# Grouped attention: DVE splits the keys in slot 0, takes the two largest logits in slot 1 and selects in slot 2

## The chip, the cores and the metric

One Trainium2 chip, one core of it. The metric is the device time of one execution of the whole program in microseconds (us). Durations of single instructions come from one profiled execution.

## What is computed

The program is a chain of two layers over 16 chunks of 512 tokens with 128 features. The change lies in the second step of the first layer: attention with 16 query heads over 4 key heads of 8 features each, then the routing of each token to two of eight experts. Cut to what matters here:

```python
q = rope((h @ Wq).reshape(b, s, 16, 8))
k = rope((h @ Wk).reshape(b, s, 4, 8))
scores = where(causal, q @ repeat(k, 4).T / sqrt(8), min)
h = clip(residual + softmax(scores) @ v @ Wo, -100, 100)
logits = rmsnorm(h) @ Wr                       # 8 experts
topv, topi = top_k(softmax(logits), 2)         # the two largest
w = sum(one_hot(topi) * topv / sum(topv))
```

## The kernel before

`grouped_attention` runs the engines by five programs written out by hand, one instruction list each, tied by semaphores. The outer loop is a pass b from -1 to 16, and a pass has eight slots s from 0 to 7. In a slot, TensorE (PE) computes the scores of one pair of heads of chunk b in three parts (`score`) and, eleven pairs ahead, the same products for the row maxima in three parts (`max_scores`); VectorE (DVE) reduces the latter (`take_max`, lines 791, 794 and 798) and ScalarE (ACT) takes exponentials of the former. Three pairs of PSUM banks go round between the two kinds, so that PE's second `score` after a `max_scores` waits until DVE has reduced it. One further bank, M, serves everything else in turn.

Around this, each slot holds pieces of work for other chunks. Those that matter here, by slot, with c2 = b + 2 the chunk whose queries and keys are prepared and r = b - 2 the chunk that is routed:

- Slot 0: GpSimd (POOL) adds the two halves of the rotated queries (`rotate`, line 636), ACT copies the keys (`copy_sum`), and DVE behind its three `take_max` splits the queries of c2 into bfloat16 parts (`split_q`, lines 779 to 783). POOL makes the third part in slot 1 (`third_q`, then `third_k`).
- Slot 1: PE multiplies the rows of chunk r with the router (`turn_h`, `route`); at the slot's end DVE copies the logits (`take_logits`, line 844) and then splits the keys of c2 (`split_k`, lines 768 to 772).
- Slot 2: DVE combines a group of the attention's output, and at the slot's end runs `choose`: the eight largest per token (line 851), their indices (line 854), the gap (line 857), and the selection matrix `sel` (line 867).
- Slot 3: PE multiplies `sel` (`rank`, line 304) between `score` parts 1 and 2, DVE runs `place`, and at the end `shift`.
- Slot 4: `max_scores` starts on the first head pair of chunk c2. Its first instruction (line 325) waits until the queries and keys of that chunk have been loaded.

The DMA queue of SyncE (SP) carries this, in order, once per pass: `store_q` (lines 1008 to 1012, waits for the split queries), `store_k` (lines 1018 to 1020, waits for the split keys), `load_q` (line 1027, waits until the queries' stores have landed), `load_k` (line 1034, waits until the keys' stores have landed), then the row maxima. In the printed rows ga_q, ga_k and g_q, g_k are buffers of the same ring of three.

Of the kernel before, what the change touches and what calls it, by code (L numbers as in the profile page):

```python
# [47 lines left out]
def grouped_attention(nc, C, XT, H, G, T, R, NB):  # L48
# [15 lines left out]
    with ExitStack() as ctx:  # L64
# [118 lines left out]
        def exists(c):  # L183
            return 0 <= c < NB
# [545 lines left out]
        def dve_program(v):  # L730
# [21 lines left out]
            def sines(c):  # L752
                v.wait_ge(qs_filled, c)
                if c > 1:
                    v.wait_ge(q_split, c - 1)
                v.tensor_tensor(rotB[:, :], M[:, :], rope[:, 1, :], ALU.mult).then_inc(sin_done, 1)

            def rotate_k(c):
                v.wait_ge(kk_filled, c)
                v.tensor_tensor(rotK[:, :], M[0:2 * KV * HD, :], k_rope[:, :], ALU.mult  # L760
                                ).then_inc(kk_done, 1)

            def split_k(c):

                v.wait_ge(sum_copied, c)
                if c > 1:
                    v.wait_ge(k_stored, 48 * (c - 1))
                v.tensor_copy(partsK[:, 0, :], restK[:, :])
                v.drain()
                v.tensor_tensor(restK[:, :], restK[:, :], partsK[:, 0, :], ALU.subtract)  # L770
                v.drain()
                v.tensor_copy(partsK[:, 1, :], restK[:, :]).then_inc(k_two, 1)

            def split_q(c):

                v.wait_ge(rotated, c)
                if c > 1:
                    v.wait_ge(q_stored, 48 * (c - 1))
                v.tensor_copy(partsQ[:, 0, :], rotA[:, :])
                v.drain()  # L780
                v.tensor_tensor(rotB[:, :], rotA[:, :], partsQ[:, 0, :], ALU.subtract)
                v.drain()
                v.tensor_copy(partsQ[:, 1, :], rotB[:, :]).then_inc(q_two, 1)

            def take_max(n, part):
                u = 3 * n + part
                v.wait_ge(max_filled, u + 1)
                h = 2 * (n % 8)
                blocks = max_banks(u).rearrange("p i (a n) -> p i a n", n=P)
                if part == 0:  # L790
                    v.tensor_reduce(bm[:, h:h + 2, 0:16:5], blocks, AX.X, ALU.max  # L791
                                    ).then_inc(max_taken, 1)
                elif part == 1:
                    v.tensor_reduce(  # L794
                        bm[:, h:h + 2, 8:14].rearrange("p i (a n) -> p i a n", n=3)[:, :, :, 0:2],
                        blocks, AX.X, ALU.max).then_inc(max_taken, 1)
                else:
                    v.tensor_reduce(bm[:, h:h + 2, 4], max_banks(u)[:, :, 0:256], AX.X, ALU.max
                                    ).then_inc(max_taken, 1)
# [18 lines left out]
            def combine(b, g):  # L818

                v.wait_ge(o_turned, 4 * b + g + 1)  # L820
                o = M[:, :].rearrange("p (a d) -> p a d", d=32)
                v.reciprocal(rsum[:, :], o[:, :, VD])
                v.drain()
                if g == 0 and b:
                    v.wait_ge(yT_filled, b)
                lanes = y[:, :, 4 * VD * g:4 * VD * (g + 1)].rearrange("p t (c d) -> p t c d", d=VD)
                shares = rsum[:, :].rearrange("p (t c) -> p t c", t=NT).unsqueeze(3)
                last = v.tensor_tensor(lanes, o[:, :, 0:VD].rearrange("p (t c) d -> p t c d", t=NT),
                                       shares.to_broadcast([P, NT, 4, VD]), ALU.mult)
                last.then_inc(o_used, 1)  # L830
                if g == 3:
                    v.wait_ge(o_used, 4 * b + 4)
                    v.sem_inc(y_ready, 1)
# [8 lines left out]
            def take_logits(r):  # L842
                v.wait_ge(logits_filled, r + 1)
                v.tensor_copy(logit[:, :, :], M[:, 0:NT * E].rearrange("p (t e) -> p t e", t=NT)
                              ).then_inc(logits_taken, 1)

            def choose(r):

                v.drain()
                for t in range(NT):  # L850
                    v.max(top[:, t, :], logit[:, t, :])
                v.drain()
                for t in range(NT):
                    v.max_index(topi[:, t, :], top[:, t, :], logit[:, t, :])
                if r >= 2:
                    v.wait_ge(ratio_ready, r - 1)
                v.tensor_tensor(gap[:, r % 2, :], top[:, :, 1], top[:, :, 0], ALU.subtract
                                ).then_inc(gap_ready, 1)
                v.drain()
                v.tensor_copy(topf[:, :, :].rearrange("p j t -> p t j"), topi[:, :, 0:2])  # L860
                v.drain()
                v.tensor_tensor(one[:, :, :, :].rearrange("p j t e -> p (j t) e"),
                                C["iota8"][:, :].unsqueeze(1).to_broadcast([P, 2 * NT, E]),
                                topf[:, :, :].rearrange("p j t -> p (j t)").unsqueeze(2
                                ).to_broadcast([P, 2 * NT, E]), ALU.is_equal)
                v.drain()
                v.tensor_tensor(sel[:, :, :], one[:, 0, :, :], one[:, 1, :, :], ALU.add
                                ).then_inc(sel_ready, 1)

            def place(r):  # L870

                v.wait_ge(ranks_filled, r + 1)
                v.tensor_tensor(pos[:, :, :], M[:, 0:NT * E].rearrange("p (t e) -> p t e", t=NT),
                                run[:, :].unsqueeze(1).to_broadcast([P, NT, E]), ALU.add)
                v.drain()
                v.tensor_tensor(run[:, :], run[:, :], M[:, NT * E:NT * E + E], ALU.add
                                ).then_inc(ranks_taken, 1)
                for j in range(2):
                    v.tensor_tensor(one[:, j, :, :], one[:, j, :, :], pos[:, :, :], ALU.mult)
                v.drain()  # L880
                v.tensor_reduce(slotf[:, :, :], one[:, :, :, :], AX.X, ALU.add)
                v.drain()
                if r >= 2:
                    v.wait_ge(scattered[r % 2], 16 * 2 * NT * (r // 2))
                v.tensor_copy(R["slot"][:, r % 2, :, :], slotf[:, :, :]).then_inc(slots_ready, 1)
# [71 lines left out]
            for b in range(-1, NB + 1):  # L957
                p, c, c2, c3, r = b - 1, b + 1, b + 2, b + 3, b - 2
                for s in range(8):
                    m = 8 * b + s + 1 + AHEAD  # L960
                    scanning = 0 <= m < 8 * NB and b > -2
                    if scanning:
                        take_max(m, 0)
                    if s == 0 and exists(p):
                        combine(p, 2)
                    if s == 2 and exists(p):
                        combine(p, 3)
                    if s == 3 and exists(r):
                        place(r)
                    if s == 4 and exists(b):  # L970
                        combine(b, 0)
                    if s == 6 and exists(b):
                        combine(b, 1)
                    if s == 7 and exists(c3):
                        sines(c3)
                    if scanning:
                        take_max(m, 1)
                    if scanning:
                        take_max(m, 2)
                    if s == 0 and exists(c2):  # L980
                        split_q(c2)
                    if s == 4 and exists(p):
                        add_out(p)
                    if s == 6 and exists(c3):
                        cosines(c3)
                    if s == 7 and exists(c3):
                        rotate_k(c3)
                    if s == 1 and exists(r):
                        take_logits(r)
                    if s == 1 and exists(c2):  # L990
                        split_k(c2)
                    if s == 2 and exists(r):
                        choose(r)
                    if s == 5 and 3 <= b + 4 < NB:
                        measure(b + 4)
                    if s == 3 and exists(c):
                        shift(c)
                    if s == 7 and b == NB - 1:
                        count_whole()
                    if s == 0 and b == NB:  # L1000
                        plan_whole()
# [2864 lines left out]
```

## Time and profile before

| | us |
|---|---|
| median of 3 runs | 3178.02 |
| their lowest and highest | 3171.54, 3179.92 |
| the profiled execution's own time | 3179.74 |
| its span, first to last instruction | 3178.0 |

The span is 1.74 us below that execution's own time. The grouped attention lies between about 538 and 1291 us of the span. Times in the timeline are from the span's start; "idle before" in brackets is the time for which the engine stood still ahead of the instruction, with what ended it; "issue" there means nothing that the profile shows. The granted clock is a share of TensorE's full 2.4 GHz; its other level is half of that.

### The profile page before, as it was taken

What the parts mean: (1) busy time and instruction counts of PE and PEld (TensorE: products, weight loads), DVE (VectorE), ACT (ScalarE), POOL (GpSimd) and SP (SyncE); (2) the same over time, 40 slices, a digit from 0 to 9 for tenths busy, and PEclk for the clock granted to TensorE, in tenths of its full rate; (3) what the DMA queues carried; (4) which work ended last, traced back from release to release, by engine and by line L of the source; (5) the groups of instructions that cost most, each with busy time, mean ns of one, the idle gap of its engine ahead of it and who ended that gap; (6) DMA issues with size and microseconds to landing.
All of it is one profiled execution on the core that took longest, in us unless ns stands there. A gap on an engine that the chain in (4) does not pass through costs nothing. (4 is left out here: it accounts for less than half of the span.)

```text
span 3178.0 us, 66212 instructions
## 1 busy us (share of the span) xinstructions
PE 2909.8 (92%) x22258; PEld 1849.4 (58%) x22258; DVE 2457.0 (77%) x6944; ACT 2327.2 (73%) x3601; POOL 2096.7 (66%) x2402
## 2 busy tenths in 40 slices
PE   6999997689898888789579999999999999999979
PEld 3555554344444444678346666666666666666658
DVE  5666665778788885567568888888888888888867
ACT  5777874356666667444279999999999999999933
POOL 5565664345565643577658877877878788778744
PEclk8999998799999999899789999999999999999989
DMA  4434444223223320585400000000000000000001
GB/s 121 130 98 121 112 104 94 59 59 69 56 61 70 69 68 24 170 276 164 135 1 1 17 1 16 2 7 11 1 17 1 17 1 17 1 17 1 1 14 41
DMA packets 151509, 178.31 MB, mean 56 GB/s; under 512 B 18619, under 2 KB 122784, under 8 KB 151076
## 3 DMA queue, kind: packets, MB, share of 16 engines
q1 hardware_dynamic: 142084, 157.14, 18.9%
q0 software_dynamic: 9088, 16.94, 1.5%
q8 instruction: 179, 2.93, 0.4%
q14 instruction: 158, 1.29, 0.1%
HBM read 99.82 MB, written 75.95 MB: 55 GB/s over the span
## 5 line engine op out<-in xcount | busy, mean ns | idle before, releaser
L3377 PE MATMUL lb_FF<-lb_h,lb_w 128*128 128x512 f32 x1024 | 501.1, 592 | 0.0
L3606 DVE TENSOR_SCALAR lb_z<-lb_M,lb_mv,lb_rstd 128x128 f32<-128x128 f32 x1024 | 344.9, 398 | 3.3 <-POOL lb_rstd L3531 3.0
L3494 ACT ACTIVATE lb_h<-lb_H,lb_prm 128x512 f32<-128x512 f32 x512 | 327.5, 699 | 2.5 <-PE lb_H L3368 2.5
L3531 POOL TENSOR_TENSOR lb_rstd<-lb_rstd,half 128x4 f32<-128x4 f32 x256 | 260.8, 1019 | 37.3 <-issue 1.3
L3362 PE MATMUL lb_H<-lb_x1s,lb_w 128*128 128x512 f32 x512 | 272.9, 533 | 0.8 <-issue 0.8
L3377 PEld LDWEIGHTS lb_FF<-lb_h,lb_w 128*128 128x128 f32 x1024 | 193.4, 189 | 89.9 <-issue 61.1
L1575 ACT ACTIVATE da_PT<-da_SY 128x1536 f32<-128x1536 f32 x128 | 185.3, 1447 | 73.5 <-PE da_SY L1424 73.3
L3598 DVE BATCH_NORM_STATS2 lb_stats<-lb_M 128x6 f32<-128x128 f32 x1024 | 226.9, 284 | 14.8 <-PE lb_M L3321 8.8
L1653 POOL TENSOR_SCALAR_AFFINE_SELECT da_PT<-da_PT 128x1024 f32<-128x1024 f32 x128 | 141.6, 1112 | 133.5 <-ACT da_PT L1570 133.5
L3363 PE MATMUL lb_H<-lb_x1s,lb_w 128*128 128x512 f32 x512 | 203.0, 397 | 0.0
L3368 PE MATMUL lb_H<-lb_x1s,lb_w 128*128 128x512 f32 x512 | 202.7, 397 | 0.0
L1436 PE MATMUL da_O<-da_PT,da_V 128*32 128x128 f32 (+2 forms) x3584 | 192.2, 326 | 2.6 <-DVE da_oT L1824 2.1
L3549 POOL CAST lb_x1s<-lb_x 128x512 fp32r<-128x512 f32 x128 | 78.3, 611 | 174.0 <-DVE lb_x L3631 174.0
L2628 POOL DMA_INDIRECT moe_ys<-moe_y,moe_dest x156 | 159.2, 1021 | 49.8 <-issue 45.8
L794 DVE TENSOR_REDUCE ga_bm<-ga_S 128x8 f32<-128x1024 f32 x128 | 156.5, 1223 | 42.9 <-PE ga_S L379 41.3
L791 DVE TENSOR_REDUCE ga_bm<-ga_S 128x8 f32<-128x1024 f32 x128 | 155.9, 1218 | 43.3 <-PE ga_S L379 42.9
L3542 POOL TENSOR_TENSOR lb_xs<-H,lb_xs 128x512 fp32r<-128x512 f32 x126 | 167.8, 1332 | 18.1
L3552 POOL TENSOR_TENSOR lb_x1s<-lb_x,lb_x1s 128x512 fp32r<-128x512 f32 x128 | 163.4, 1276 | 20.8 <-issue 20.8
L3563 POOL TENSOR_TENSOR lb_y<-lb_ao,H 128x512 f32<-128x512 f32 x128 | 165.4, 1292 | 16.2 <-ACT lb_ao L3481 14.0
L3575 POOL TENSOR_TENSOR lb_y<-lb_ff,lb_x 128x512 f32<-128x512 f32 x128 | 165.1, 1290 | 8.3 <-PE lb_M L3321 5.8
L3475 ACT ACT_TABLE_LOAD x131 | 168.1, 1283 | 2.3
L3452 ACT ACT_TABLE_LOAD x128 | 164.2, 1283 | 2.3
(514 smaller groups left out, 8774.8 us busy)
## 6 DMA issues: line engine op xcount, KB each, us to landing
moe_w<-experts_dram SPq DMA_DIRECT2D x39, 384.0 KB, 3.1
da_qT<-da_stq SPq DMA_DIRECT2D x64, 192.0 KB, 3.9
da_kT<-da_stk SPq DMA_DIRECT2D x64, 192.0 KB, 3.4
moe_x<-moe_xs SPq DMA_DIRECT2D x39, 260.0 KB, 3.6
tc_g<-moe_ys SPq DMA_DIRECT2D x32, 256.0 KB, 3.3
ga_q<-ga_stq SPq DMA_DIRECT2D x20, 384.0 KB, 5.9
lb_split<-moe_parts SPq DMA_DIRECT2D x8, 896.0 KB, 6.1
da_stq<-da_parts SPq DMA_DIRECT2D x16, 384.0 KB, 2.4
```

The costliest lines, as they stand in the source:

```text
L1436: last = pe.matmul(O[32 * c:32 * c + 32, q0:q0 + cols], V[:, (n // 4) % 2, j, 2 * (n % 4) + c % 2, :], PT[:, (2 * n + c // 2) % RING, c % ...
L1575: act.activation(PT[:, n % RING, :, 512:HEAD_COLS], SY[:, :, :].rearrange("p a n -> p (a n)").rearrange("p (i n) -> p i n", i=2), ACT.Exp, ...
L3362: pe.matmul(H[:, k % 2, :], w1[:, 0, k, :], x1s[:, 0, :], start=True, stop=False)
L3363: pe.matmul(H[:, k % 2, :], w1[:, 1, k, :], x1s[:, 0, :], start=False, stop=False)
L3368: pe.matmul(H[:, k % 2, :], w1[:, 0, k, :], x1s[:, 1, :], start=False, stop=True).then_inc(h_filled, 1)
L3377: pe.matmul(FF[:, :], w2[:, k, :], h[:, k, :], start=(k == 0), stop=(k == KC - 1)).then_inc(ff_filled, 1)
L3475: act.preload_act_table_set("gelu_apprx_tanh_and_others")
L3494: act.activation(h[:, k, :], H[:, k % 2, :], ACT.Gelu_apprx_tanh, bias=col(FB1 + k, i)).then_inc(h_ready, 1)
L3531: pool.tensor_tensor(out[:, :], out[:, :], C["half"][:, 0:NT], ALU.pow).then_inc(done, 1)
L3542: pool.tensor_tensor(part_of_x(i, 1), state(i), part_of_x(i, 0).bitcast(F32), ALU.subtract).then_inc(xs_ready, 1)
L3598: v.bn_stats(stats[:, t, :], M[:, t * P:(t + 1) * P])
L3606: last = v.tensor_scalar(z[:, t, :], M[:, t * P:(t + 1) * P], mv[:, t, 0:1], rstd[:, t:t + 1], ALU.subtract, ALU.mult)
```

## The change

On DVE alone, three things move. `split_k` goes from the end of slot 1 to the end of slot 0, directly behind `split_q`. The search for the largest logits and their indices goes from `choose` at the end of slot 2 to `take_logits` at the end of slot 1, behind a drain of its own. `choose` keeps the gap, the selection and a drain ahead of them. No instruction is dropped; one drain per routed chunk is added. The lists of the other engines and of SP stay.

```diff
                 v.tensor_copy(logit[:, :, :], M[:, 0:NT * E].rearrange("p (t e) -> p t e", t=NT)
                               ).then_inc(logits_taken, 1)
+                v.drain()
+                for t in range(NT):
+                    v.max(top[:, t, :], logit[:, t, :])
+                v.drain()
+                for t in range(NT):
+                    v.max_index(topi[:, t, :], top[:, t, :], logit[:, t, :])
 
             def choose(r):
 
                 v.drain()
-                for t in range(NT):
-                    v.max(top[:, t, :], logit[:, t, :])
-                v.drain()
-                for t in range(NT):
-                    v.max_index(topi[:, t, :], top[:, t, :], logit[:, t, :])
                 if r >= 2:
                     v.wait_ge(ratio_ready, r - 1)
...
                         rotate_k(c3)
+                    if s == 0 and exists(c2):
+                        split_k(c2)
                     if s == 1 and exists(r):
                         take_logits(r)
-                    if s == 1 and exists(c2):
-                        split_k(c2)
                     if s == 2 and exists(r):
                         choose(r)
```

## Rows read from the trace of the kernel before

**Rows 1.** The page, part 1: busy time, share of the span, instructions.

```profile
PE 2909.8 (92%) x22258; PEld 1849.4 (58%) x22258; DVE 2457.0 (77%) x6944; ACT 2327.2 (73%) x3601; POOL 2096.7 (66%) x2402
```

**Rows 2.** Waits of PE from 600 to 1176: sum in us, times, longest.

```profile
PE ga_S L325 <- issue: 21.6, 12, 4.5
PE ga_S L355 <- DVE ga_bm L791: 14.4, 16, 1.7
PE ga_M L304 <- DVE g_sel L867: 13.7, 11, 1.7
```

**Rows 3.** Timeline of pass 10, from its slot 0 to its slot 4.

```profile
1042.15 0.43 DVE L779 CAST ga_partsQ<-ga_rotA 128x512 bf16<-128x512 f32 x1 [1.02 <-POOL ga_rotA L636]
...
1043.76 1.22 DVE L791 TENSOR_REDUCE ga_bm<-ga_S 128x8 f32<-128x1024 f32 x1
...
1045.03 0.28 PE L355 MATMUL ga_S<-ga_q,ga_k 51*128 51x256 bf16 x2 [1.10 <-DVE ga_bm L791]
...
1046.06 1.80 SPq L1012 DMA_DIRECT2D ga_stq<-ga_partsQ  x1
...
1046.72 0.40 DVE L768 CAST ga_partsK<-ga_restK 32x512 bf16<-32x512 f32 x1
...
1048.29 1.21 DVE L791 TENSOR_REDUCE ga_bm<-ga_S 128x8 f32<-128x1024 f32 x1
...
1049.63 0.32 SPq L1018 DMA_DIRECT2D ga_stk<-ga_partsK  x1
...
1050.98 0.89 SPq L1027 DMA_DIRECT2D g_q<-ga_stq  x2
...
1052.04 0.83 SPq L1034 DMA_DIRECT2D g_k<-ga_stk  x2
...
1052.09 0.37 DVE L851 MAX8 g_top<-g_logit 128x8 f32<-128x8 f32 x4
...
1053.10 0.15 DVE L857 TENSOR_TENSOR g_gap<-g_top 128x4 f32<-128x4 f32 x1
...
1054.22 0.18 PE L304 MATMUL ga_M<-g_sel,g_matsb 128*128 128x32 bf16 x1 [1.27 <-DVE g_sel L867]
...
1059.97 0.39 PE L325 MATMUL ga_S<-identb,half_masks 64*128 64x256 bf16 x4 [1.89 <-issue]
```

**Rows 4.** DMA issues from 600 to 1170: KB each, median us to landing.

```profile
ga_k<-ga_stk SPq DMA_DIRECT2D x18, 192.0 KB, 7.2
...
ga_stq<-ga_partsQ SPq DMA_DIRECT2D x13, 128.0 KB, 2.7
```

**Rows 5.** Timeline: PE at slot 4 of pass -1 and of pass 1.

```profile
580.71 0.61 PE L325 MATMUL ga_S<-identb,half_masks 64*128 64x256 bf16 x4 [8.68 <-DMA ga_k<-ga_stk]
...
663.85 0.61 PE L325 MATMUL ga_S<-identb,half_masks 64*128 64x256 bf16 x4 [4.30 <-issue]
```

**Rows 6.** Stretches: length, busy PE, PEld, DVE, ACT, POOL, clock, DMA, GB/s.

```profile
690.16:1175.70 485.54, 433.66 (x5396) 224.40 (x5396) 400.69 (x862) 309.73 (x740) 283.86 (x385) 0.95 0.29 65
929.84:954.87 25.03, 24.55 (x312) 12.09 (x312) 20.86 (x37) 17.58 (x45) 15.96 (x20) 1.00 0.09 27
1059.97:1086.56 26.59, 26.11 (x312) 12.71 (x312) 20.36 (x35) 16.77 (x43) 14.94 (x20) 0.94 0.08 26
957.76:968.27 10.51, 9.42 (x113) 6.06 (x114) 8.61 (x28) 6.02 (x13) 5.75 (x11) 0.84 0.66 156
1045.03:1054.22 9.19, 7.91 (x112) 5.16 (x113) 8.42 (x28) 6.03 (x14) 4.43 (x10) 1.00 0.59 157
870.58:882.64 12.06, 10.84 (x112) 6.98 (x113) 8.84 (x28) 6.15 (x14) 6.41 (x12) 0.72 0.64 146
```

**Rows 7.** Timeline of the last pass: DVE's logits and their search.

```profile
1279.99 0.19 DVE L844 COPY g_logit<-ga_M 128x32 f32<-128x32 f32 x1 [0.98 <-PE ga_M L295]
...
1283.17 0.37 DVE L851 MAX8 g_top<-g_logit 128x8 f32<-128x8 f32 x4 [0.20 <-DVE ga_y L828]
```

More of the change, by code:

```diff
@@ L845, in take_logits @@
                               ).then_inc(logits_taken, 1)
-            def choose(r):
                 v.drain()
@@ L854, in choose @@
                     v.max_index(topi[:, t, :], top[:, t, :], logit[:, t, :])
+            def choose(r):
+                v.drain()
                 if r >= 2:
```

## The prediction

> **What bounds the kernel now.** I read the page first: PE is busy for 92% of the span and DVE for 77% [rows 1], so that neither alone explains a stage. The edit touches only the grouped attention, so I went to the waits of PE inside that stage, then to the timeline of one pass, then to the DMA issues, and last to stretches with their granted clock. Three waits of PE stand out [rows 2]. The largest is at line 325, where `max_scores` meets a new chunk in slot 4: 21.6 us in 12 of 13 passes, put down to "issue". The next are PE in slot 1 on DVE's `take_max` (14.4 us) and PE in slot 3 on the selection matrix (13.7 us in 11 passes, 1.25 each).
>
> What is behind "issue"? In pass -1 the same wait is put down to the load of the keys [rows 5]. In pass 10, SP issues the two key loads from 1052.04 on, the second some 0.4 us later, and a key load lands 7.2 us after its issue [rows 4]: 1059.65, against PE's start at 1059.97 [rows 3]. So PE waits for the keys. They are late because DVE splits them only at 1046.72, at the end of slot 1.
>
> So a pass is a loop with a gate. Counted from line 779 of pass 10 (1042.15), PE resumes in slot 1 at 2.88, reaches `rank` at 12.07, arrives at the gate at 15.93 and passes it at 17.82 [rows 3]. From the gate to the next pass's line 779 it is 25.03 us at full clock in pass 7 and 26.59 us in pass 10, whose clock was 0.94 there [rows 6]. The mean pass from 2 to 12 takes 485.54 / 11 = 44.14 us [rows 6].
>
> **The change part by part.** *Keys in slot 0.* The split of the keys occupies DVE for 1.57 us (1046.72 to 1048.29, the next `take_max`) [rows 3]. Placed at 1043.76 it delays all three `take_max` of slot 1 by that much, and PE's wait in slot 1, on the first of them, grows from 1.10 to 2.67: PE resumes at 4.45. Behind it on DVE stand those reductions and the logits; behind them wait PE's `score` part 2 and `route`, and ACT's last exponentials. The keys' copy by ACT is an earlier piece of the same slot and has the 1.61 us of the query split as cover; without cover its lateness would add to this delay.
>
> *Search in slot 1.* From line 851 to line 857 it is 1.01 us [rows 3]; with the new drain I take 1.1 (below, a drain costs nothing and it is 1.0; above, 0.3 like the gaps between the dependent steps of `choose` would make it 1.3). It takes the place of the 1.57 us at the end of slot 1, so that slot 2's first `take_max` is late by 1.57 - 1.57 + 1.1 = 1.1 or so on DVE's own account, while PE offers its input 1.57 late. In slot 2, PE is therefore the one that sets the pace, at +1.57. At the end of slot 2, DVE is about 1.33 behind, the search is gone, and the gap comes at 1.33 - 1.01 = 0.32 later than now. The selection is ready at 12.07 + 0.33 = 12.4.
>
> *Slot 3.* PE needs 9.19 us from its start in slot 1 to `rank`, 1.27 of them wait [rows 3, 6]. 4.45 + 7.92 = 12.37: the wait on the selection disappears, as PE itself comes 1.57 later. Up to the gate it is another 3.86 us, so PE arrives at 16.26 rather than 15.93. Alone, the regrouping on DVE thus moves a wait from slot 3 to slot 1 and costs 0.33 us a pass. ACT's ratio and POOL's row weights come later by the same amount, and no other engine waits on those before the scatter.
>
> *What the earlier keys trigger.* From line 768 to the first store it is now 2.91 us [rows 3]; from 1043.76 that gives 1046.67. SP is then still in `store_q`, whose last issue starts at 1046.06. The key stores take 1.35 us of SP's time, but `load_q` behind them also needs the queries landed, 2.7 us after their last issue [rows 4], at 1048.76. So the loads start at 1048.8, not 1050.98: 2.15 us earlier. Bounds: 1.75 if SP's last query store always takes the 1.80 us of this pass, 2.9 if the landing were no limit. The gate opens at 17.82 - 2.15 = 15.67, at most 16.07: before PE is there.
>
> *The clock.* A longer stop may drop it. From PE's start in slot 1 to `rank`, pass 10 had clock 1.00 and took 9.19 us, pass 8 had 0.84 and 10.51, pass 6 had 0.72 and 12.06 [rows 6]. Without the wait on the selection these are 7.92, 9.26 and 10.81, so the arrivals are 16.26, 17.57 and 19.12. Passes of 41.3, 42.6 and 44.15 us follow with 25.03 us behind the gate, as pass 7 has where the gate held PE little. The Trainium skill (TensorE: Matmul & The Clock Gate, section "HAM oscillation — how this bites in real kernels") warns that a wait which recurs at every tile throttles PE anew at every tile. By that rule every pass would pay; the trace agrees for passes 6 and 8, not for pass 10, which waited as long. By the rule alone the whole would come to 3153, by pass 10's row to 3137.
>
> *The sum.* I take low clock once in ten of passes 2 to 13 (42.6, each 1.54 less) and the longer kind in two (no gain): -15.4. Passes -1 to 1 route nothing and wait 8.68, 4.5 and 4.30 at the gate [rows 2, 5]; more than the 1.57 by which PE can come later, so each gains the 2.15 of the load: -6.5. In the last three passes no keys are split. In the last, the logits are there at 1279.99 but the search starts at 1283.17, behind `combine` [rows 7]: 1.0 us leaves the chain. The same 1.0 leaves pass 14's selection wait, and pass 15 I cost at nothing, as ACT's exponentials cover it: -2.0. The profiled execution took 3179.74: less 23.9 it is 3156. (The median of the runs is 1.7 lower; I leave that in the range.)
>
> **The rivals.** About 0.3%, 9.5 us, is what a measurement of this kernel tells from no change.
>
> *No low clock in slots 1 and 2.* 41.3 a pass: 12 x 2.84 = 34, with the other 8.5 it is 3137. For it speaks pass 10; against it that the wait is 2.4 times as long.
>
> *The longer low clock in every pass*, as in pass 6, whose wait of 1.7 was the longest of its kind [rows 2]: 44.15, so passes 2 to 13 gain nothing and only 8.5 remain: 3171. It speaks for it that this is the one pass with a longer wait, against it that the clock was low from the wait's end on there, so may have been cause as much as effect.
>
> *The load does not come forward*, because the stores of queries and keys now share the queue and land later. The gate stays at 17.82: passes of 42.85 (low clock ahead of it) to 44.41, about 0.5 gained in each, and nothing in the first three: 3172. Against it: stores and loads of one pass never overlap, since `load_q` waits for the landing.
>
> *Slower: the clock falls twice a pass.* The slot 1 wait brings the long kind (44.15) and another stretch falls low behind the gate, at 26.59 - 25.03 = 1.56 more [rows 6]: 45.7, or +18.8 in twelve passes, less 8.5: 3190. It decides from a mean clock of about 0.89 over passes 2 to 12, against 0.95 now. Against it: behind the gate it was the stop at the gate that preceded the fall, and that stop goes.
>
> **How the numbers follow.** The forecast's case (3145 to 3168 by itself) has 0.50, no low clock 0.10, the longer low clock 0.22, the unmoved load 0.08, the slower case 0.10. The faster ones are the first two, 0.60; the next two lie within 0.3%, 0.30; slower 0.10. The range leaves out the slower case and most of the 3137 case: 3141 to 3180.
>
> **What would show it.** The wait of PE in slot 1 near 2.7 us (line 355 on line 791); no wait on the selection before `rank`; "issue" at line 325 close to nothing from pass 2 on and about 2 us shorter in passes -1 to 1; line 1034 about 7.7 us behind line 779, from 9.89; passes near 42.6 us. The forecast is wrong if the gate's wait stays, if the clock over passes 2 to 12 leaves 0.92 to 0.98, or if a later stage takes back what this one gains.

## The result, and the profile after

The changed kernel takes 3185.85 us (median of 7 runs, 3181.76 to 3195.03) against 3175.28 (7 runs, 3171.24 to 3179.92): a ratio of 1.0034, 95% interval 1.0021 to 1.0047. It is slower by 10.6 us, just beyond what a measurement tells from no change; forecast were 3156 and a range of 3141 to 3180. The profiled execution, the longest of the seven, took 3195.03 (span 3193.3) against 3179.74.

First the waits of PE in the changed kernel from 600 to 1176, as in [rows 2].

```profile
PE ga_S L355 <- DVE ga_bm L791: 49.8, 26, 3.7
PE ga_S L325 <- DVE ga_bm L794: 7.5, 14, 0.7
...
PE ga_M L304 <- DVE g_sel L868: 0.4, 1, 0.4
```

Two of the three waits of [rows 2] are gone, as forecast: "issue" at line 325 (21.6 us) and the selection (13.7, now 0.4). But the wait in slot 1 has grown from 14.4 to 49.8 us, by 35.4, which is as much as the two together. The timeline of pass 10 shows how it is made up (from line 844 on, lines after the moved search stand one lower than before, so load_k is line 1035 and the selection 868).

```profile
1052.15 0.43 DVE L779 CAST ga_partsQ<-ga_rotA 128x512 bf16<-128x512 f32 x1 [0.99 <-POOL ga_rotA L636]
...
1053.75 0.41 DVE L768 CAST ga_partsK<-ga_restK 32x512 bf16<-32x512 f32 x1
1053.92 1.26 POOL L640 TENSOR_TENSOR ga_partsQ<-ga_rotB,ga_partsQ 128x512 bf16<-128x512 f32 x1 [1.80 <-DVE ga_partsQ L783]
1054.24 1.48 DVE L770 TENSOR_TENSOR ga_restK<-ga_restK,ga_partsK 32x512 f32<-32x512 f32 x1
...
1056.13 1.21 DVE L791 TENSOR_REDUCE ga_bm<-ga_S 128x8 f32<-128x1024 f32 x1
...
1057.40 0.28 PE L355 MATMUL ga_S<-ga_q,ga_k 51*128 51x256 bf16 x2 [3.43 <-DVE ga_bm L791]
...
1061.31 0.79 SPq L1035 DMA_DIRECT2D g_k<-ga_stk  x2
...
1066.91 0.18 PE L304 MATMUL ga_M<-g_sel,g_matsb 128*128 128x32 bf16 x1
...
1070.16 0.39 PE L325 MATMUL ga_S<-identb,half_masks 64*128 64x256 bf16 x4 [0.55 <-DVE ga_bm L794]
...
1070.61 0.39 PE L325 MATMUL ga_S<-identb,half_masks 64*128 64x256 bf16 x4
...
1073.85 0.28 PE L355 MATMUL ga_S<-ga_q,ga_k 51*128 51x256 bf16 x2 [0.50 <-DVE ga_bm L791]
...
1096.49 0.43 DVE L779 CAST ga_partsQ<-ga_rotA 128x512 bf16<-128x512 f32 x1 [1.01 <-POOL ga_rotA L636]
```

PE resumes in slot 1 at 5.25 from line 779 (forecast 4.45) after a stop of 3.43 (forecast 2.67), reaches `rank` at 14.76 without a wait, and the pass takes 44.34. The gate is the instruction at 1070.61, and it starts without a wait. (The one at 1070.16, on the same line, belongs to the `score` ahead of it and waits for a reduction of DVE.) In pass -1 the gate still holds PE, for 5.87 us instead of 8.68 [rows 5]:

```profile
579.86 0.61 PE L325 MATMUL ga_S<-identb,half_masks 64*128 64x256 bf16 x4 [5.87 <-DMA ga_k<-ga_stk]
```

Next stretches of the changed kernel, columns as in [rows 6]: passes 2 to 12; from PE's start in slot 1 to `rank` in passes 10, 9 and 8 (that of pass 8 begins 0.04 us early); from `rank` to the next line 779 in pass 10.

```profile
684.10:1185.17 501.07, 443.84 (x5396) 232.68 (x5396) 409.86 (x862) 310.36 (x740) 284.00 (x385) 0.93 0.28 63
1057.40:1066.91 9.51, 9.43 (x113) 6.09 (x113) 7.29 (x25) 5.01 (x11) 6.17 (x12) 0.82 0.90 173
1011.93:1022.53 10.60, 10.51 (x112) 6.94 (x113) 7.39 (x25) 5.01 (x11) 6.18 (x12) 0.72 0.89 163
965.02:977.11 12.09, 11.64 (x113) 7.04 (x114) 7.43 (x25) 5.34 (x12) 6.21 (x12) 0.65 0.78 145
1066.91:1096.49 29.58, 27.93 (x360) 13.74 (x360) 24.99 (x49) 20.95 (x53) 17.27 (x22) 1.00 0.10 27
```

Read the column of the granted clock (0.93 for passes 2 to 12, from 0.95): PE is busy nearly without a gap behind the stop, yet it needs 9.51 to 12.09 us for the same work, since part of it runs at the lower level of 1.2 GHz. The eleven passes take 501.07 instead of 485.54: 45.55 each, not 44.14. Passes -1 to 1 fell from 127.55 to 120.93, and the time from pass 13's line 779 to the start of the last addition of the output (line 839) from 114.41 to 111.27. Together the attention, up to that addition, ends 6.3 us later (1296.44, from 1290.11).

The remainder is at the other end of the program, in code that the diff does not touch. The last stage, from the last use of `lb_H` to the end of the span, takes 157.1 us instead of 149.5. Here are two groups of its instructions, first before, then after (busy time, mean of one, idle time ahead):

```profile
L3038 POOL TENSOR_TENSOR ff_r<-ff_r 128x512 f32<-128x512 f32 x32 | 44.2, 1395 | 29.1 <-ACT ff_r L3020 29.0
L3064 DVE TENSOR_SCALAR ff_xn<-XT,ff_mv,ff_rstd 128x128 f32<-128x128 f32 x56 | 17.9, 383 | 10.5 <-POOL ff_rstd L3030 10.5
```

```profile
L3039 POOL TENSOR_TENSOR ff_r<-ff_r 128x512 f32<-128x512 f32 x32 | 38.4, 1204 | 29.6 <-ACT ff_r L3021 29.6
L3065 DVE TENSOR_SCALAR ff_xn<-XT,ff_mv,ff_rstd 128x128 f32<-128x128 f32 x56 | 24.6, 502 | 11.9 <-POOL ff_rstd L3031 11.9
```

The same 56 instructions of DVE take 24.6 us, not 17.9, while POOL's squares got shorter. The timeline of the changed kernel there shows why:

```profile
3133.04 1.84 DVE L3065 TENSOR_SCALAR ff_xn<-XT,ff_mv,ff_rstd 128x128 f32<-128x128 f32 x4 [0.89 <-POOL ff_rstd L3031]
...
3133.73 1.06 POOL L3039 TENSOR_TENSOR ff_r<-ff_r 128x512 f32<-128x512 f32 x1 [0.73 <-ACT ff_r L3021]
...
3134.93 0.66 PE L2965 MATMUL ff_M<-ident,ff_xn 128*128 128x128 f32 x4 [0.54 <-DVE ff_xn L3065]
```

POOL's square falls beside DVE's four normalisations (1.84 us). In the kernel before it fell behind them (1.12 for the same four) and beside DVE's own squares (line 3087):

```profile
3093.63 1.12 DVE L3064 TENSOR_SCALAR ff_xn<-XT,ff_mv,ff_rstd 128x128 f32<-128x128 f32 x4 [0.68 <-POOL ff_rstd L3030]
...
3094.66 2.13 DVE L3087 TENSOR_TENSOR ff_r<-ff_r 128x512 f32<-128x512 f32 x2
...
3094.76 2.93 POOL L3038 TENSOR_TENSOR ff_r<-ff_r 128x512 f32<-128x512 f32 x2 [1.17 <-ACT ff_r L3020]
```

PE waits on line 3065 ten times, for 8.4 us in all, where it waited twice, for 2.7.

### The profile page after: what moved, and what is told of

It is laid out like the page before. It is cut to its first block and busy times, and to the rows that moved or that the text cites. A ratio compares the mean times of both kernels' runs of the same rounds, so it can differ in the third digit from the quotient of the medians.

```text
span 3193.3 us, 66227 instructions
## 1 busy us (share of the span) xinstructions
PE 2920.9 (91%) x22258; PEld 1856.9 (58%) x22258; DVE 2474.6 (77%) x6944; ACT 2327.9 (73%) x3601; POOL 2090.4 (65%) x2402
## 5 line engine op out<-in xcount | busy, mean ns | idle before, releaser
L3599 DVE BATCH_NORM_STATS2 lb_stats<-lb_M 128x6 f32<-128x128 f32 x1024 | 226.8, 283 | 13.9 <-PE lb_M L3322 8.9
L794 DVE TENSOR_REDUCE ga_bm<-ga_S 128x8 f32<-128x1024 f32 x128 | 156.2, 1220 | 36.9 <-PE ga_S L379 36.6
```

Source lines behind the costliest of these rows:

```text
L3599: v.bn_stats(stats[:, t, :], M[:, t * P:(t + 1) * P])
```

## The experiments

**Half of the change each.** First the search alone, moved to slot 1; the keys are split behind it.

```diff
                               ).then_inc(logits_taken, 1)
+                v.drain()
+                for t in range(NT):
+                    v.max(top[:, t, :], logit[:, t, :])
+                v.drain()
+                for t in range(NT):
+                    v.max_index(topi[:, t, :], top[:, t, :], logit[:, t, :])
             def choose(r):
                 v.drain()
-                for t in range(NT):
-                    v.max(top[:, t, :], logit[:, t, :])
-                v.drain()
-                for t in range(NT):
-                    v.max_index(topi[:, t, :], top[:, t, :], logit[:, t, :])
```

> Kernel before with the search alone moved to slot 1, ahead of the key split, which stays in slot 1. If the cost of the change lies in the key split's new place (position theory) or in the overlap of its subtraction with POOL's third query part (overlap theory), this kernel lacks both: line 770 stays at 0.68 us, the stop of PE in slot 1 stays at 1.1, the wait on the selection before rank shrinks. But the keys are then split 1.1 us later, so the gate in slot 4 opens 1.1 us later and passes 2 to 13 take about 45.2 instead of 44.1: 3175 + 13 - 2 = 3186 (ratio 1.003). If it is the search in slot 1 that costs (rival), the loss comes without a later gate: a new stop of PE in slot 2 and a gate with no longer a wait.

3207.59 us (4 runs, 3202.44 to 3211.13), ratio 1.0093 (1.0076 to 1.0110), and so slower still than the 3186 expected. Timeline of pass 10 (its line 779 is at 1063.95): key split, load of the keys, gate.

```profile
1069.70 0.40 DVE L768 CAST ga_partsK<-ga_restK 32x512 bf16<-32x512 f32 x1
...
1075.02 0.83 SPq L1035 DMA_DIRECT2D g_k<-ga_stk  x2
...
1083.00 0.61 PE L325 MATMUL ga_S<-identb,half_masks 64*128 64x256 bf16 x4 [2.78 <-issue]
```

The loads start at 11.07 (9.89 before) and the gate opens at 19.05 (17.82). That is the forecast's loop of keys and gate, turned against the kernel: 1.2 us later in, 1.2 us later out. The passes grew by 2.57 (46.71), so the stop of 2.78 cost more than its lateness; the clock over passes 2 to 12 was 0.91. No new stop came in slot 2 (PE's waits on line 794 sum to 8.5 us, 8.6 before), so the rival, which put the loss on the search itself, falls.

Then the split alone, moved to slot 0.

```diff
                     if s == 0 and exists(c2):
                         split_q(c2)
...
+                    if s == 0 and exists(c2):
+                        split_k(c2)
                     if s == 1 and exists(r):
                         take_logits(r)
-                    if s == 1 and exists(c2):
-                        split_k(c2)
```

> Kernel before with the key split alone moved to slot 0; the search stays in slot 2. Position and overlap theories: stop of PE in slot 1 of 3.45 us as in the changed kernel, line 770 at 1.48, no wait at the gate from pass 0 on, and the wait on the selection before rank back at about 1, so that passes take up to 1.1 us more than in the changed kernel: 45.4 to 47, in all 3186 to 3200. The search rival: this kernel is as fast as before or faster, since it gains the loads and pays no search in slot 1.

3203.21 us (4 runs), ratio 1.0083 (1.0066 to 1.0099), 3 us above the range expected. The waits of PE:

```profile
PE ga_S L355 <- DVE ga_bm L791: 50.1, 26, 4.1
PE ga_M L304 <- DVE g_sel L867: 11.8, 11, 1.4
```

The stop in slot 1 is the changed kernel's, 3.44 to 3.46 in most passes; the selection is late as well, and no wait at the gate is left. Each half alone loses about 30 us, both together 10.6: the early keys repair the late gate of the one, the early search the late selection of the other, and neither undoes the stop in slot 1.

**The third part of the queries out of the way.** In the changed kernel, POOL's `third_q` (line 640) runs beside DVE's subtraction of the keys (line 770). Here it also waits for the key split.

```diff
             def third_q(c):
                 pool.wait_ge(q_two, c)
+                pool.wait_ge(k_two, c)
```

> Changed kernel, with POOL's third query part held until the key split is done, so that it no longer runs beside the split's subtraction. Overlap theory: line 770 falls from 1.48 to 0.68, PE resumes in slot 1 at 4.45 after line 779 instead of 5.25, and passes 2 to 13 lose 0.8 each at least: 3186 - 10 = 3176; more (3165) if the low clock in slots 1 and 2 becomes shorter with the stop. Rival, that the slow subtraction has another cause than POOL's instruction beside it: line 770 stays at 1.48 and the time at 3186. The query stores come about 1.5 us later, which the gate has room for (3 us in the changed kernel).

3181.49 us (10 runs, 3172.95 to 3185.63), ratio 1.0023 (1.0011 to 1.0034). Pass 10 and the stretch of passes 2 to 12:

```profile
1041.35 0.68 DVE L771 TENSOR_TENSOR ga_restK<-ga_restK,ga_partsK 32x512 f32<-32x512 f32 x1
...
1042.66 1.15 POOL L641 TENSOR_TENSOR ga_partsQ<-ga_rotB,ga_partsQ 128x512 bf16<-128x512 f32 x1 [3.44 <-DVE ga_partsK L773]
...
1043.71 0.28 PE L355 MATMUL ga_S<-ga_q,ga_k 51*128 51x256 bf16 x2 [2.66 <-DVE ga_bm L792]
```

```profile
682.24:1172.40 490.16, 441.80 (x5396) 232.24 (x5395) 401.36 (x863) 310.40 (x740) 283.22 (x385) 0.93 0.29 65
```

The subtraction is back at 0.68, and the stop at 2.66: the forecast's figure to 0.01. The other kernels of this study bear it out in every pass: the subtraction takes 0.68 where it doesn't meet `third_q`, and 1.48 or 1.49 (once 1.13) where it does. A pass falls by 1.0 to 44.56, the attention ends at 1282.51. But the clock stays at 0.93: even the stop that was forecast brings the lower level in every pass. The attention is 13.9 us shorter than the changed kernel's, the whole 9.4 by the profiled executions (3185.63 against 3195.03) and 4.4 by the medians; single runs of either kernel lie over 12 us apart, which is too much to place the difference.

**The keys in the middle.** The changed kernel, but with the key split behind the first reduction of slot 1, whose result lets PE go on.

```diff
                     if scanning:
                         take_max(m, 0)
+                    if s == 1 and exists(c2):
+                        split_k(c2)
...
-                    if s == 0 and exists(c2):
-                        split_k(c2)
```

> Changed kernel, with the key split in slot 1 behind the first of the three reductions instead of ahead of it. PE's second score part in slot 1 waits only for that first reduction. Position theory: the stop of PE there is 1.1 again, a second one of about 1.2 comes at the start of slot 2, the subtraction no longer meets POOL's third query part (0.68), the keys still come early enough for the gate (1.2 us later than in the changed kernel), and passes take 42 to 42.6: 3150 to 3160, faster than before by 0.5 to 0.8%. Rival, that DVE's total work in slots 0 to 3 sets the pass whatever its order: 44 or more, 3175 or more.

3173.76 us (10 runs), ratio 0.9995 (0.9985 to 1.0005): no change, where 3150 to 3160 were expected. Two stops of about one us (1.08 in slot 1, 1.01 at the start of slot 2) stand in place of one of 3.43, yet passes 2 to 12 take what they took before, and the clock is again 0.93:

```profile
683.26:1168.80 485.54, 442.40 (x5396) 227.46 (x5395) 401.77 (x863) 310.13 (x740) 282.92 (x385) 0.93 0.28 65
```

The pass of 44 is what the rival asked for, but this run doesn't show its reason, DVE's total work: the clock from the stop to `rank` was 0.71 in passes 6 to 13, and the runs below part the two. The attention ends 10.4 us earlier (1279.73), from passes -1 to 1 and the last three; of that, the last stage takes back 6.6 (156.1).

**The attention by itself, and the clock.** The next four kernels leave out everything behind the grouped attention and write out its result, so that nothing later blurs the comparison. The third has 13 extra multiplications where PE would stand still (operands shortened here).

```diff
                     if scanning:
                         max_scores(m, 1)
+                    if s == 1 and exists(r) and exists(c2):
+                        bank_free()
+                        for _ in range(13):
+                            pe.matmul(M[:, :], identb, half_masks, start=True, stop=True)
                     if attending:
                         score(n, 2)
```

In the fourth, POOL's rotation of the queries moves, and the keys are split in the middle as above.

```diff
                 for s in range(8):
-                    if s == 0 and exists(c2):
+                    if s == 0 and b == -1:
                         rotate(c2)
+                    if s == 7 and exists(c3):
+                        rotate(c3)
```

> The kernel before, cut off behind the grouped attention: the expert tiles, the collection, the linear blocks and the ternary stage are left out and the attention's result is written out. It is the base for the next three. In the whole kernel's profile that stage ends at 1290.11 us of the span, so some 1293 to 1300 us here, and passes 2 to 12 near 44.1 us each.

> The changed kernel, cut off at the same place. Theory 1 (the loss lies in the attention itself: the key split beside POOL's third part of the queries, the lower clock behind the longer stop, and the cover that the gate's wait gave to DVE): the stage ends 6.3 us later in the whole kernel's profile, so +4 to +9 us against the kernel before cut in the same way, PE's stop in slot 1 of 3.4 us and the subtraction of the key split at 1.48 us as in the whole kernel. Rival (the loss is made by the later stages, whose lengths differ from run to run): within 2 us of the other one.

> The changed kernel cut off, with 13 extra multiplications of 128x512 into the bank M, whose product nothing reads, in slot 1 of the passes that route and prepare keys, where PE would stand still for 3.4 us. They take about as long as that stop (13 times 0.21 to 0.25 us at full clock), so they delay nothing much by themselves. Theory 1a (the stop drops the clock, and the half clock costs 1.5 to 3 us up to rank): the granted clock stays at 1.00 from slot 1 to rank, rank comes about 13.2 us after line 779 instead of 14.8 to 16, and a pass takes some 42.8 us: 25 to 35 us less than the changed kernel cut off. Rival 1b (DVE sets the pace behind the stop, PE merely follows it): clock 1.00, but the pass stays within 0.5 us of the changed kernel's.

> The kernel cut off, with the keys split between the first and second reduction of slot 1 as in the run before this series, and in addition POOL's rotation of the queries moved from slot 0 to slot 7, ahead of the scatter, so that DVE finds it done at line 779. Theory: DVE's wait of 1.0 us ahead of line 779 goes, its work of slots 0 and 1 comes a little earlier and the pass falls by 0.5 to 1.0 us: 8 to 20 us less than the kernel before cut off. Rival: the wait was covered, as PE sets the pace from slot 5 to slot 0 and POOL in slot 7 now delays the scatter: no gain against the split in the middle, whose whole kernel took as long as the kernel before.

| cut off behind the attention | us (4 runs each) | passes 2 to 12, us each |
|---|---|---|
| before | 1306.9 (1302.88 to 1308.74) | 44.06 |
| changed | 1312.27 (1310.83 to 1315.55) | 45.55 |
| changed, extra multiplications | 1283.26 (1279.81 to 1285.07) | 43.13 |
| keys in the middle, early rotation | 1263.01 (1253.75 to 1269.01) | 41.33 |

The base is 7 us beyond the 1293 to 1300 expected, as writing out the result takes 15 us behind the last addition; its passes are as expected. The attention itself accounts for 5.4 of the 10.6 us. And PE's 13 useless multiplications make it 29.0 us shorter: the theory of the clock holds, the rival (DVE sets the pace) falls. Keys in the middle and early rotation together brought 43.9 us against the kernel before, where 8 to 20 were expected: the expectation counted DVE's wait of 1.0 us and not the clock, which is 0.99 over passes 2 to 12.

**The same in whole kernels.** The changed kernel with the 13 multiplications, then the rotation moved in the kernel before, in the changed one, and in the one with the keys in the middle.

> The changed kernel, whole, with the 13 extra multiplications in slot 1. Theory (the clock after the longer stop is what the change pays with): the attention cut off by itself became 29.0 us shorter by them, so 3185.85 - 29.0 = 3157, between 3150 and 3163, which is faster than the kernel before. Rival (the later stages hold what the attention gains or loses back): 3170 or more.

> The kernel before, whole, with one edit: POOL rotates the queries in slot 7 instead of slot 0, so that DVE no longer waits 1.0 us ahead of line 779. Theory (a pass pays for the stops of PE and for the half clock behind each): DVE comes 1.0 us earlier against PE, the stop in slot 1 (1.06) goes, the gate opens 1.0 earlier, and the low clock falls below 2 us a pass: passes of 41.5 to 42.5, 3140 to 3155. Rival (the gain of 44 us came from the keys' new place between the reductions, the rotation only adds to it): passes of 43 or more, 3160 to 3174.

> The changed kernel, whole, with POOL's rotation of the queries in slot 7. Theory: the 1.57 us of the key split in slot 0 plus 0.8 for its neighbour on POOL still stop PE for 2.0 to 2.7 us in slot 1, so the clock still falls there: passes of 43.5 to 44.5, 3160 to 3175, well behind the kernel before with the same edit. Rival (the order on DVE doesn't matter once DVE has no wait): within 5 us of the kernel before with the same edit.

> Whole: the change's early search, the keys split between the first and the second reduction of slot 1, and the rotation in slot 7. The attention cut off was 43.9 us shorter than the one before, so 3173.9 - 43.9 = 3130, between 3122 and 3138. Rival (the later stages give part of it back, as where the keys alone were moved to the middle): 3140 to 3155.

With the multiplications: 3163.22 us (10 runs), ratio 0.9962 (0.9950 to 0.9974), 0.2 us above the theory's range and 7 below the rival's. Its stretches: from the first instruction behind the stop to `rank` in pass 10 (the window lies 0.2 us early at both ends; the stretch itself takes 7.97), and passes 2 to 12.

```profile
1034.80:1042.76 7.96, 7.77 (x112) 5.12 (x112) 7.09 (x26) 4.64 (x11) 6.36 (x12) 1.00 0.95 189
683.52:1158.19 474.67, 446.56 (x5528) 229.68 (x5539) 407.82 (x863) 308.50 (x740) 284.14 (x385) 1.00 0.29 67
```

7.97 us at clock 1.00 for what takes 9.51 at 0.82 and 10.60 at 0.72: PE goes on at 5.25 behind DVE's first instruction of the split, as in the changed kernel, only it stood idle for 0.53 us ahead of that and not for 3.43. One pass, 6, still fell (9.5 us at 0.82). Against the changed kernel's 45.55 a pass takes 43.15.

The early rotation in the kernel before: 3171.6 us (10 runs), ratio 0.9987 (0.9971 to 1.0002), where 3140 to 3155 were expected; it lies in the rival's range, with passes of 43.35. Its wait on the selection, and then its gate in pass 10, say why: the stop in slot 1 shrank to 0.3 us, but keys and selection stayed late against PE.

```profile
PE ga_M L304 <- DVE g_sel L869: 13.3, 11, 1.6
```

```profile
1051.42 0.40 PE L325 MATMUL ga_S<-identb,half_masks 64*128 64x256 bf16 x4 [1.90 <-issue]
```

In the changed kernel: 3179.39 us (10 runs), ratio 1.0014 (1.0001 to 1.0028), 4 us above the range expected and 8 behind the kernel before with the same edit; the stop in slot 1 shrank to 2.39 and the passes to 44.45, with the clock at 0.93 still.

With the keys in the middle: 3143.31 us (4 runs, 3141.07 to 3150.56), ratio 0.9908 (0.9880 to 0.9935), faster than both kernels. It lies in the rival's range: the attention ends 42.4 us earlier than before (1247.7), and the last stage, at 156.2, takes 6.7 back. Its passes 2 to 12, and the largest waits of PE from 600 to 1130:

```profile
681.23:1138.89 457.66, 422.82 (x5370) 218.47 (x5372) 400.78 (x862) 308.07 (x738) 282.38 (x385) 0.99 0.30 69
```

```profile
PE ga_S L325 <- DVE ga_bm L796: 17.5, 26, 2.0
PE ga_S L379 <- ACT ga_PT L545: 10.3, 26, 0.5
PE ga_S L355 <- DVE ga_bm L793: 5.2, 10, 1.1
PE ga_M L304 <- DVE g_sel L870: 5.1, 11, 1.0
```

The keys in the middle alone gave nothing a pass, the rotation alone 0.79, both 2.53: PE's stops have become short (0.2 to 0.7 us, but for three in the eleven passes), the gate holds it seldom, and the clock is 0.99. DVE's list is the same as with the keys in the middle alone, so DVE's total work doesn't set the pass of 44 there.

**The last stage.** Its length had gone with the place of the search: 149.5 to 150.9 us in three kernels with the search in `choose`, 155.3 to 157.4 in seven with the search in slot 1. The two differ in something else too, one more drain on DVE per routed chunk. The attention routes 15 of the 16 chunks, so that is 15 drains in all (the pages list 66212 and 66227 instructions), not the sixteen of the expectations below.

```diff
             def choose(r):

                 v.drain()
+                v.drain()
```

> The kernel before with one more drain in `choose`, so that DVE's list has as many instructions as the changed kernel's (one more in each routed chunk, sixteen in all) and everything else is in its old place. In the profiles so far the last stage took 149.5 to 150.9 us in the three kernels whose search stands in `choose`, and 155.3 to 157.4 us in the seven whose search stands in slot 1 with its own drain. Theory A (the longer list of DVE, by where its instructions fall, puts the last stage into its slower pattern): 155 to 157 us there, and the whole 5 to 8 us slower than the kernel before: 3179 to 3186. Theory B (it is the search's place): 149 to 151 us, the whole within 4 us of the kernel before.

> The changed kernel with one more drain in `choose` (sixteen more in all). Theory A (where DVE's instructions fall decides the pattern of the last stage): it may go back to 149 to 151 us, or stay; if the run before this one shows 155 to 157 and this one 150, the count decides. Theory B: 155 to 158 us, as the search has the same place. The attention itself should stay within 3 us of the changed kernel's 1296.4 in both.

The kernel before with the drain: 3181.47 us (10 runs), ratio 1.0016 (1.0001 to 1.0031), 3.4 us above the kernel before, last stage 156.9. The changed kernel with a further one: 3179.33 us (10 runs), ratio 1.0010 (0.9994 to 1.0026), last stage 149.2. The normalisations of DVE in the one and in the other:

```profile
L3065 DVE TENSOR_SCALAR ff_xn<-XT,ff_mv,ff_rstd 128x128 f32<-128x128 f32 x56 | 24.5, 500 | 11.9 <-POOL ff_rstd L3031 11.9
```

```profile
L3066 DVE TENSOR_SCALAR ff_xn<-XT,ff_mv,ff_rstd 128x128 f32<-128x128 f32 x56 | 17.8, 380 | 10.5 <-POOL ff_rstd L3032 10.5
```

Both last stages flipped with the search left where it was: theory A, though the first kernel lost less than the 5 to 8 us expected. The passes stayed near what they were (44.01 and 45.29), but the attentions ended 6.4 and 3.9 us earlier than without the drain, further from the changed kernel's 1296.4 than the 3 us expected. To see whether it is the number alone, the same line was added to the fastest kernel.

> The kernel with the early search, the keys split between the reductions and the rotation in slot 7, with one more drain in `choose`. If the number of drains alone puts the last stage into one of its two patterns, the last stage falls from 156.2 to 149 to 151 us and the whole from 3143.3 to about 3137 (3132 to 3142). Rival (the pattern depends on more than that, such as the attention's length): 155 to 157 us, the whole 3141 to 3151.

3134.0 us (4 runs, 3126.88 to 3138.16), ratio 0.9865 (0.9842 to 0.9887); last stage 150.9. It is the fastest version of this study. In all thirteen whole kernels the length goes with the number of added drains: 149.5 to 150.9 us with none (three kernels), 155.3 to 157.4 with 15 (eight), 149.2 and 150.9 with 30. So 15 drains, some 1700 us ahead of it, decide on 5 to 8 us in the last stage. What in them does so (the place of the later instructions in DVE's list, or a shift in their times) stays open.

## Why the prediction was wrong

*Right.* The loop of keys and gate: the loads start 7.7 us behind line 779 in most passes (9.16 in pass 10), and from pass 0 on PE doesn't wait at the gate. The wait on the selection is gone. Passes -1 to 1 gained 6.6 (forecast 6.5), in part by luck: not 2.15 each but 1.87, 2.37 and 2.39, and in passes 0 and 1 no wait at the gate is left, where the forecast counted on one. Passes 14 to 16 gained 2.5 (forecast 2.0), counted from PE's `turn_h` in slot 1: 1.0 in pass 14 and nothing in pass 15, as forecast, and 1.5 in the last, where the logits' search follows 0.28 us behind their copy, not 3.18 [rows 7].

*The step that failed* is the size of passes 2 to 13, "-15.4": measured are +14.9 (15.5 in passes 2 to 12, -0.6 in pass 13). Three of its terms were too small, by nearly the same amount. For passes 2 to 12 the forecast's mean pass is 44.14 - 15.4 / 12 = 42.86; measured are 45.55. By parts, where PE resumes, from there to `rank`, and from there to the next line 779:

| | forecast | measured | with PE kept busy (whole) |
|---|---|---|---|
| PE resumes in slot 1 | 4.45 | 5.24 | 5.25 |
| from there to `rank` | 9.52 | 10.65 | 8.24 |
| `rank` to the next pass | 28.89 | 29.66 | 29.67 |
| pass | 42.86 | 45.55 | 43.15 |

*The clock.* From PE's start in slot 1 to `rank` the forecast is 1.13 short. Of that, 0.81 is the clock: the forecast gave it 9.52 - 7.92 = 1.60 a pass, and it costs 10.65 - 8.24 = 2.41. The other 0.32 is there with PE kept busy too (8.24, not 7.92). The text took 9.26 for ten of twelve passes, from pass 8 of before, and let pass 10, with its stop of 1.10, speak for less [rows 3, 6]. Behind a stop of 2.4 to 3.7, in most passes 3.43 to 3.45, every pass from 2 to 13 fell to the lower level: passes 10 to 13 as in the 9.51 above, passes 2 to 9 between the 10.60 and the 12.09. In the eleven passes the clock costs 26 us (501.07 against 474.67), and 22.6 between the medians: without it the change would have been faster than the kernel before. The rival with the longer low clock in every pass had this mechanism and was given 0.22. The sign that the text set for the clock, 0.92 to 0.98 over passes 2 to 12, did not catch it: 0.93 lies inside. The rule of the Trainium skill (TensorE: Matmul & The Clock Gate, section "HAM oscillation — how this bites in real kernels") that the text weighed is that a wait which recurs at every tile throttles anew at every tile. The trace agrees for this stop, with a clock of 0.64 to 0.82 from its end to `rank` in each of passes 2 to 13; the short stops of the fastest kernels recur as well, and there the clock was 0.99.

*The stop*: PE resumes at 5.24, 0.79 later than the forecast. The split was priced at its 1.57 of slot 1, but in slot 0 it meets POOL's `third_q`, and the subtraction takes 1.48 instead of 0.68; without the meeting the stop is 2.66. The prediction named `third_q` nowhere: it moved DVE's work past an engine's work that starts from the same place, and looked only at who waits. The Trainium skill (SBUF — State Buffer, section "🔬 SBUF: two separate sides") has a rule for it: DVE with two operands in SBUF and GpSimd share a port pair, of which the first to start keeps the other out until it is done. Here POOL was first and ended at 1055.18; 0.68 behind it would be 1055.86, and DVE ended at 1055.72: the trace agrees, to 0.14 us. POOL's own 1.26, against 1.15 where they don't meet, such a lock that POOL holds doesn't explain.

*The cover.* Behind `rank` it is 29.66, not 3.86 + 25.03. The 25.03 are pass 7's, behind a gate that held PE for 0.41 us:

```profile
929.84 0.39 PE L325 MATMUL ga_S<-identb,half_masks 64*128 64x256 bf16 x4 [0.41 <-issue]
```

In pass 10 of the changed kernel it is 3.70 up to the gate (1070.61) and 25.88 behind it. Without a hold at the gate PE waits 0.50 us on DVE's reduction (1073.85), which pass 7 doesn't: the larger part of the 0.85 more. That the hold had given DVE time to get ahead is read from these rows; no run tests it by itself. With PE kept busy it is the same 29.67, so it is not the clock's.

*What was not in the sum.* The last stage is longer by 7.6 us in the profiles. The text had named "a later stage takes back" among what would make it wrong, with no price. With the attention's 5.4 by itself that makes 13, against 10.6 (6.7 to 14.9 by the interval) measured.

*The slower rival* gave 45.7 a pass and 3190, close to what came, but by a second low stretch behind the gate. There is none: from `rank` on the clock was 1.00.

## What to carry over

Before moving work on an engine to another slot, look at what the other engines do there, and price the moved work by its duration beside them (here 1.48 us beside POOL, 0.68 alone). A stop that is moved is not a stop of the same price: with stops of mostly 0.2 to 0.7 us the clock stayed at 0.99, with two of 1.0 or one of 2.4 to 3.4 in each pass it was 0.93, so let the work that TensorE waits for go first and take away the rest of its waits too. And compare the stages that were not touched as well: a few instructions more can shift a distant pattern by as much as the change itself is worth.

## What was unexpected

DVE's 32x512 subtraction took 1.48 us beside POOL's 128x512 subtraction, 0.68 alone; POOL's took 1.26 and 1.15. TensorE gained 29.0 us in the attention by 128x512 multiplications that nobody reads. Fifteen drains on DVE moved the last stage from 149.5 to 156.9 us, and thirty took it back to 149.2 and 150.9.
